# Eight batches of attention as one block without barriers, and one test of the score bound at its end

## The reference, cut to what matters

```python
q = _layernorm(q, q_gamma, q_beta); k = _layernorm(k, k_gamma, k_beta)
dots = jnp.einsum('bhnd,bhne->bhde', k, v)
out = jnp.einsum('bhnd,bhde->bhne', q, dots) * (1.0 / n)
...
scores = jnp.einsum('bhnd,bhmd->bhnm', q, k) / sqrt(Dh)
attn = jax.nn.softmax(scores, axis=-1)
sa = jnp.einsum('bhnm,bhmd->bhnd', attn, v)
```

## Time and profile before

| what | value |
|---|---|
| device time, three runs | 1817.12, 1822.64, 1822.80 us; median 1822.64 |
| the profiled execution, its span | 1855.2 us |
| TensorE, VectorE, ScalarE, POOL busy in it | 1449.7, 1112.1, 883.7, 575.7 us |
| before the first front | 18.8 us |
| front 0 | 18.8 to 130.5 us |
| attention of batches 0 to 6 | 130.5 to 1431.7 us |
| attention 7 | to 1536.2 us |
| store 7 | to 1563.5 us |
| routing and experts | to 1855.2 us |

### The profile page before, as it was taken

How to read it: one execution, slowest core, us unless ns; L and a number is a source line. 1 busy time by engine, 2 the same in 40 slices (tenths; PEclk the granted TensorE clock), 3 DMA queues, 4 the chain that set the end, 5 groups by cost and what they waited for, 6 DMA issues and landing times. The chain is left out here.

```text
span 1855.2 us, 28644 instructions
## 1 busy us (share of the span) xinstructions
PE 1449.7 (78%) x10308; PEld 902.9 (49%) x10308; DVE 1112.1 (60%) x2276; ACT 883.7 (48%) x1281; POOL 575.7 (31%) x1142
## 2 busy tenths in 40 slices
PE   5669998989698969996999699969998995213565
PEld 3435655555455536554655465536555554112444
DVE  3226765666476747564667476657665884764553
ACT  2235564656465636564656466646565772000111
POOL 1303410452035203520352035204520221035664
PEclk7788998999899989998999899989999997557777
DMA  2152015101610161005300630053004303012221
GB/s 73 36 120 63 1 40 134 56 1 37 143 51 1 29 144 58 1 6 141 85 1 1 138 92 1 1 127 102 2 1 108 99 2 98 0 44 81 90 89 60
DMA packets 73757, 109.47 MB, mean 59 GB/s; under 512 B 12410, under 2 KB 56443, under 8 KB 73595
## 3 DMA queue, kind: packets, MB, share of 16 engines
q1 hardware_dynamic: 66409, 90.47, 19.6%
q0 software_dynamic: 6144, 16.79, 2.8%
q10 hardware_dynamic: 1042, 0.01, 0.0%
HBM read 20.98 MB, written 25.43 MB: 25 GB/s over the span
## 5 line engine op out<-in xcount | busy, mean ns | idle before, releaser
L843 ACT ACTIVATE probs<-scores 128x1024 f32<-128x1024 f32 x512 | 519.3, 1023 | 265.0 <-PE scores L622 171.7
L622 PE MATMUL scores<-query_stack,key_stack 128*128 128x256 f32 x2048 | 410.5, 325 | 110.4 <-issue 86.0
L1062 DVE TENSOR_TENSOR prob_sum<-prob_sum,probs 128x512 f32<-128x512 f32 x640 | 454.8, 759 | 16.2 <-ACT probs L843 16.2
L622 PEld LDWEIGHTS scores<-query_stack,key_stack 128*128 128x128 f32 x2048 | 294.8, 196 | 256.8 <-issue 188.0
L640 PE MATMUL acc<-probs,v_sb 128*32 128x256 f32 x4096 | 331.0, 396 | 8.8 <-ACT probs L843 8.8
L862 POOL TENSOR_TENSOR attn_T<-acc_sb 128x256 f32<-128x256 f32 x64 | 61.9, 966 | 645.8 <-DVE acc_sb L1047 634.2
L663 PE MATMUL shared<-w_sb,chan 128*128 128x512 f32 (+1 forms) x512 | 188.6, 504 | 5.0 <-DVE chan L974 5.0
L1047 DVE RECIPROCAL acc_sb<-acc_sb 128x256 f32<-128x256 f32 x64 | 111.6, 1744 | 107.6 <-ACT acc_sb L833 107.6
L1182 PE MATMUL y_ps<-w_sb,zT 128*128 128x256 f32 x256 | 90.1, 488 | 76.8 <-DVE result L1341 51.4
L1351 ACT ACTIVATE zT<-zT_ps 128x256 f32<-128x256 f32 x64 | 24.6, 384 | 257.4 <-PE zT_ps L1173 209.3
L640 PEld LDWEIGHTS acc<-probs,v_sb 128*32 128x32 f32 x4096 | 88.4, 109 | 111.6 <-issue 43.0
(11 more groups left out here) (164 smaller groups left out, 2046.4 us busy)
## 6 DMA issues: line engine op xcount, KB each, us to landing
query_stack<-hi SPq DMA_DIRECT2D x128, 128.0 KB, 2.5
key_stack<-hi SPq DMA_DIRECT2D x128, 128.0 KB, 2.6
x_sb<-in_x_dram SPq DMA_DIRECT2D x8, 1024.0 KB, 8.2
key_stack<-lo SPq DMA_DIRECT2D x64, 128.0 KB, 2.5
query_stack<-lo SPq DMA_DIRECT2D x64, 128.0 KB, 2.5
v_sb<-v_next SPq DMA_DIRECT2D x16, 512.0 KB, 3.7
out_dram<-resid SPq DMA_DIRECT2D x16, 512.0 KB, 3.3
tokens_scratch<-resid SPq DMA_DIRECT2D x16, 512.0 KB, 4.2
```

Source lines behind the costliest of these rows:

```text
L622: last = pe.matmul(score_ps[u % 2][:, QB * r:QB * (r + 1)], key_stack[:, HG * g + r, P * kt:P * (kt + 1)], query_stack[:, HG * g + r, QB * ...
L843: act.activation(probs[:, u % 3, :], score_ps[u % 2][:, :], ACT.Exp, scale=DH ** -0.5) \
L1062: dve.tensor_tensor(total[:, part], probs[:, (u - 1) % 3, part] if kt == 1 else total[:, part], probs[:, u % 3, part], ALU.add).then_inc(s ...
```

## The change

All segments stand in one block. A Segment says which batch it attends to, which front and which store run beside it; lay_out deals the steps of every segment over its 64 slots and numbers the units on over all batches (0 to 511). build_segments makes the code of all engines from this plan: written out for the eight batches, without a loop. Semaphores count on over the batches, where they had been cleared. What the barrier had kept apart is now kept apart by waits: the first scores of a batch for its copies of group 0, SP's copies of group 1 for the last weighing of the batch before, agg for attn_T, the copies of ScalarE into hi and lo for the DMAs that read them. x of the next front is loaded after lin of this one. The last block of a batch is summed, copied, inverted and divided in slots 1 to 4 of the next batch, as any other. The maxima of the norms are kept for all batches and the bound is made once, in the segment of the last store. After the block the flag is tested once, and where it is set all batches are computed again, with the shift. The three DMAs that fill rows 96 to 127 stand in the small block ahead. head_mask has one copy in place of two.

```diff
@@ -102,7 +103,7 @@
              ("square", 3, 0), ("proj", 0, 1), ("proj", 1, 1), ("norms", 3, 0), ("square", 0, 1), ("v", 0),
              ("norms", 0, 1), ("square", 1, 1), ("v", 1), ("norms", 1, 1), ("proj", 2, 1), ("v", 2),
              ("square", 2, 1), ("proj", 3, 1), ("norms", 2, 1), ("square", 3, 1), ("v", 3), ("norms", 3, 1),
-             ("rest", 2), ("bound_rows",), ("rest", 2), ("bound",), ("rest", 2)]
+             ("rest", 2)]
     wanted = {"store": store, "attend": attend, "front": front, "rest": attend and front}
     part = {k: "store" for k in store_part} | {k: "attend" for k in attend_part} | {"rest": "rest"}
     return [x for x in steps if wanted[part.get(x[0], "front")]]
...
                .then_inc(sems["stack_rows"], 1)
             dve.wait_ge(sems["stack_rows"], 3)
+
+        @block.sync
+        def _(sp):
+            sp.wait_ge(sems["stack_rows"], 3)
+            for target, source in ((key_stack[MAX_ROW:MAX_ROW + 1], one_row),
+                                   (key_stack[MAX_ROW + 1:P], zero_rows[1:P - MAX_ROW]),
+                                   (query_stack[MAX_ROW:P], zero_rows)):
+                sp.dma_start(target.bitcast(F32), source.unsqueeze(1).to_broadcast([source.shape[0], H, N])) \
+                  .then_inc(sems["stack_rows"], 16)
+            sp.wait_ge(sems["stack_rows"], 3 + 48)
 
     def ended():
 
@@ -382,39 +385,22 @@
         nc.gpsimd.sem_clear(range(nums[0], nums[-1] + 1))
         nc.all_engine_barrier()
 
-    def attended(b, **work):
-
-        needs_shift = nc.values_load(shifted[0:1, 0:1], min_val=0, max_val=1)
-        with nc.If(needs_shift > 0):
+    ended()
+    build_segments(nc, env, [Segment(front=0)] +
+                   [Segment(attend=b, front=b + 1 if b + 1 < B else None, store=b - 1 if b else None)
+                    for b in range(B)] + [Segment(store=B - 1, last=True)], first_x_loaded=True, guard=True)
+    ended()
+
+
+    needs_shift = nc.values_load(shifted[0:1, 0:1], min_val=0, max_val=1)
+    with nc.If(needs_shift > 0):
+        with nc.Fori(0, B) as b:
+            build_segments(nc, env, [Segment(front=b)], first_x_loaded=False, guard=False)
+            ended()
             build_shift(nc, env)
             ended()
-        build_batch(nc, env, b, attend=True, **work)
+            build_segments(nc, env, [Segment(attend=b), Segment(store=b)], first_x_loaded=False, guard=False)
             ended()
-
-    ended()
-    build_batch(nc, env, 0, front=True)
-    ended()
-    attended(0, front=True)
-    with nc.Fori(1, B - 1) as b:
-        attended(b, front=True, store=True)
-    attended(B - 1, store=True)
-    build_batch(nc, env, B, store=True)
-    ended()
...
+def lay_out(segments, guard):
...
+        steps = order(seg.has("attend"), seg.has("front"), seg.has("store"))
+        if not guard:
+            steps = [x for x in steps if x[0] not in ("square", "norms")]
+        elif seg.last:
+            steps = [("bound_rows",), *steps, ("bound",)]
+        dealt = (UNITS if seg.has("front") else 4 * T) if seg.has("attend") else 1
+        dealt = spread(steps, dealt) + [[]] * (UNITS - dealt if seg.has("attend") else 0)
+        for u, slot in enumerate(dealt):
...
+
+            if not first_x_loaded and all_fronts:
+                sp.dma_start(x_sb[:, :, :], env["x_v"][segments[0].front, :, :, :]).then_inc(s["x_loaded"], 16)
+            for n, seg in enumerate(segments):
+                if seg.has("attend"):
+
+                    await_count(sp, "weighed", UNITS * seg.attends)
+                    if seg.earlier_front:
+                        for h in range(2):
+                            for j in range(2, 4):
+                                await_read(sp, seg.earlier_front, "proj", j, h)
+                    copy_group(sp, env, 1)
+                    if seg.earlier_front:
+                        for k in range(T // 2 - 2, T // 2):
+                            await_read(sp, seg.earlier_front, "v", k)
+                    copy_v(1)
...
+                if seg.has("front"):
+                    if n + 1 < len(segments) and segments[n + 1].has("front"):
+                        for t in range(T - 2, T):
+                            await_read(sp, seg, "lin", t)
+                        sp.dma_start(x_sb[:, :, :], env["x_v"][segments[n + 1].front, :, :, :]) \
+                          .then_inc(s["x_loaded"], 16)
+                    if seg.has("attend"):
+                        sp.wait_ge(s["weighed"], UNITS * seg.attends + UNITS // 2)
+                    for h in range(2):
+                        for j in range(2):
+                            await_read(sp, seg, "proj", j, h)
+                    copy_group(sp, env, 0)
+                    for k in range(T // 2 - 2, T // 2):
+                        await_read(sp, seg, "v", k)
+                    copy_v(0)
+            await_count(sp, "x_loaded", 16 * (all_fronts - x_preloaded))
...
             def scores(u):
-                g, qb, kt = u // (NQB * T), u // T % NQB, u % T
-                if u == UNITS // 2:
-                    pe.wait_ge(s["group_copied1"], STACK_DMAS)
+                a, g, qb, kt = u // UNITS, u % UNITS // (NQB * T), u // T % NQB, u % T
+                if u % UNITS == 0:
+                    await_count(pe, "group_copied0", STACK_DMAS * (a + segments[0].has("front")) if all_fronts else 0)
+                if u % UNITS == UNITS // 2:
+                    pe.wait_ge(s["group_copied1"], STACK_DMAS * (a + 1))
...
                 if kind == "agg":
-                    if at[0] == T - QB // P:
-                        pe.wait_ge(s["attn_ready"], late)
+                    pe.wait_ge(s["attn_ready"], G * NQB * seg.stores + NQB * (G - 1) + at[0] // (QB // P) + 1)
                     last = product(ps[:, 0:C], [(attn_T[:, c, tok[at[0]]], waggT[:, c, :]) for c in range(CH)])
...
-                        act.wait_ge(s["group_copied1"], STACK_DMAS)
+                    ps = await_full(act, seg, *st)
+                    if at[0] == 0:
+                        await_count(act, "group_copied1", STACK_DMAS * seg.groups)
                     read(act.activation(z2T[:, :, P * at[0]:P * (at[0] + 1)],
...
-
-            if late:
-                divide(-1)
-            for u, slot in enumerate(slots):
-                for st in slot:
-                    step(st)
-                if attend and u > T and u % T == 4:
+                elif kind == "head_scale" and at[0] < seg.pool_quarters:
+                    scale_heads(pool, seg, at[0]).then_inc(s["head_scaled"], 1)
+
+            for n, slot in enumerate(plan):
+                u = slot.unit
+                if units and u is None and n and plan[n - 1].unit == units - 1:
+                    divide(units // T - 1)
+                for st in slot.steps:
+                    step(*st)
+                if u and u > T and u % T == 4:
                     divide(u // T - 1)
 
```

More of the change, by code:

```diff
@@ L25 @@
 from contextlib import ExitStack
+from dataclasses import dataclass, field
 F32 = mybir.dt.float32
@@ L67, in spread @@
     rests = sum(x[1] for x in steps if x[0] == "rest")
-    share = sum(WORK[x[0]] for x in steps if x[0] != "rest") / (slots - rests)
+    share = sum(WORK[x[0]] for x in steps if x[0] != "rest") / (slots - rests) or 1.0
     done, out = 0.0, [[] for _ in range(slots)]
@@ L122, in bank_uses @@
 def bank_uses(slots):
-    return {s: k for k, s in enumerate(s for slot in slots for s in slot if s[0] not in BANKLESS)}
+    return {s: k for k, s in enumerate(s for slot in slots for s in slot if s[1][0] not in BANKLESS)}
 def hybrid_kernel(nc, x, w0, q_gamma, q_beta, k_gamma, k_beta, w1, wagg, bagg, wgate, wexp, out):
@@ L505, in _, with has, groups @@
                 pool.wait_ge(s[f"max_row_in{g}"], 16)
-def build_batch(nc, env, b, front=False, attend=False, store=False):
-    s = env["sems"]
-    nxt = b + 1 if attend else b
-    steps = order(attend, front, store)
-    dealt = (UNITS if front else 4 * T) if attend else 1
-    slots = spread(steps, dealt) + [[]] * (UNITS - dealt if attend else 0)
-    use = bank_uses(slots)
+@dataclass(eq=False)
+class Segment:
+    front: object = None
+    attend: object = None
+    store: object = None
+    last: bool = False
+    fronts: int = 0
+    attends: int = 0
+    stores: int = 0
+    scaled_before: int = 0
+    scaled_last_before: int = 0
+    pool_quarters: int = 0
+    slots: list = field(default_factory=list)
+    earlier_front: object = None
+    def has(self, part):
+        return {"front": self.front, "attend": self.attend, "store": self.store}[part] is not None
+    @property
+    def groups(self):
+        return self.attends + self.has("attend")
@@ new lines @@
+@dataclass(eq=False)
+class Slot:
+    unit: object
+    steps: list
+def lay_out(segments, guard):
+    fronts = attends = stores = scaled = scaled_last = 0
+    earlier_front = None
+    plan = []
+    for seg in segments:
+        seg.fronts, seg.attends, seg.stores = fronts, attends, stores
```

(40 more changed lines are left out.)

464 lines of the change are left out of this document (219 added, 245 removed).

## The result

| | before | after |
|---|---|---|
| device time, median of 12 runs each (lowest to highest) | 1826.26 us (1817.12 to 1831.94) | 1837.14 us (1832.53 to 1838.51) |
| ratio, 95% interval | | 1.0059 (1.0042 to 1.0075) |
| span of the profiled execution | 1855.2 us | 1833.3 us |

The changed kernel is 10.9 us slower; forecast was 16.9 us faster. The direction is wrong, and the forecast is 28 us off.

A forecast was written before the change was run, and what follows sets the result against it. TensorE was taken to set the pace in the attention. The terms +65.5 + 24.6 + 5 - 81.0 - 21 - 7 - 3 = -16.9 took 1822.6 us to 1805.7, range 1795 to 1817.

The forecast's parts named there:

- the start: Ahead of the first front: waiting for the three DMAs that fill stack rows moves it from 18.87 to 84.3, +65.5 us.
- the gaps: Seven boundaries between batches: barrier, clearing, flag load and branches leave the path before the scores, -81.0 us.
- agg 6: TensorE's step in slot 5, batches 1 to 6: waits 4.1 us each for POOL's division of attn_T, +24.6 us.
- the drain and the fresh start: Around each of seven batch boundaries: work running out and starting anew goes, 3 us each (0 to 5), -21 us.
- the new deal: Steps dealt over 64 slots with four fewer of rest, said to give the filling at boundaries; no size of its own.
- The first attention and front 0: Batch 0's scores need only the front's last copies, and the wait for x falls away: -7 us (0 to -10).
- The end: Flag loaded and branched on once after the last store, +5 us; one score bound and no barrier there, about -3.
- The copies on SP: Copies into the stacks for the next batch: group 0 costs 0, group 1 costs 0, up to 3 us a batch.

The follow-up runs named there:

- rests_back: The changed kernel with 6.8 slots without steps at the end of a batch instead of 2; 1824.35 us, 0.9995 of the kernel before.
- rests_close: The changed kernel with 6.8 slots without steps and each batch's last query block closed in slots 0 and 1 of the next; 1802.99 us.
- before_unrolled: The kernel before with its loop over batches 1 to 6 written out, barriers, flag and branches kept; 1774.96 us, 0.9734 of the kernel before.
- rows_32: The changed kernel with key_stack's rows 96 to 127 filled by one transfer of 32 partitions instead of 1 and 31; 1781.44 us.

## Why the prediction was wrong

**Right: the start.** +65.5 forecast, +66.0 in the profile, 65 and 67 in the two kernels that price it. The reading of the earlier trace rows (one engine, landing near 84) holds.

**Right: the gaps.** -81.0 forecast; all seven are gone, and writing out the loop gives 48.5 us in ordinary runs, where the profile has 51.5.

**Right as a mechanism, wrong in this kernel: agg 6.** The prediction said "The place of agg 6 (slot 5) and the work ahead of it stay." Only the first half holds. 24.6 forecast, 24.8 with the old deal, 4.2 in after.

**The step that failed: batches 1 to 6.** The step is the term of 3 us a boundary for "the drain and the fresh start", together with the new deal of the steps, which stood at nothing in the sum. Forecast for these batches: six gaps (81.0 less the 6.55 before batch 1, 74.5), six times 3 us of drain and fresh start, and the 24.6 of agg 6: -67.9. Measured: -39.9. These 28.0 us are the error (26.5 in profile time over all, -16.9 against +9.6). They come in two parts:

- *Drain and fresh start, -21 for seven boundaries (-18 for six).* With the old deal (rests_back) batches 1 to 6 shrink by 46.3 us; gaps and the wait for attn_T give -74.5 + 24.8 = -49.7. So what is left for the term is +3.4, not -18: 21.4 us missed. Its lower bound of 0, "if the work merely moves", was nearer. No run shows the 3 us a boundary, which were my estimate; what the runs showed in their place is this remainder.

  The +3.4 is a remainder and holds other waits that came and went: TensorE's for POOL's lo (20.4 us before) are gone, its waits for probs grew from 24.2 to 47.4. In sum its idle time beside the gaps and the wait for attn_T stayed the same (73.1 before, 1077.0 - 979.0 - 24.8 = 73.2), and its busy time rose by 3.3 us instead of falling.

  With the wait at agg 6 removed as well (rests_close) the remainder is +4.9 (-69.6 against -74.5). There TensorE's busy time did fall, by 12.1 us (975.7 to 963.7), so the clock does come back (0.99 in the batch shown; 0.94 and 0.97 in those of before, gaps included). But its idle time without the gaps rose by 16.9 us (before 1123.3 - 975.7 - 74.5 = 73.1; rests_close 1053.7 - 963.7 = 90.0), at exps that wait for VectorE's sums (TensorE's waits for probs 53.7 us, where they were 24.2) and at VectorE's resid and lin_out (15.4 and 17.0).

  In after the busy time didn't even fall (980.9): the granted clock was 0.51 in two stretches of batch 3, nearly as low as the 0.50 behind a gap of the kernel before (497.76 to 499.76 us). The first begins behind the wait of 2.21 us before agg 5, the second at the end of the wait of 5.25 us for POOL's lo:

```profile
735.30:742.20 6.90, 6.27 (x31) 3.98 (x30) 5.06 (x15) 3.02 (x4) 1.46 (x2) 0.51 0.99 282
...
817.20:820.70 3.50, 3.33 (x18) 2.22 (x19) 0.62 (x1) 2.18 (x3) 0.07 (x1) 0.51 0.00 0
```

- *The new deal, 0 in the sum.* I had written that fewer slots of rest give "the filling". They gave collisions: 6.4 us in batches 1 to 6 and 4.6 in batch 0, 11.7 in the runs. That is a net figure, since the new deal took 20.6 us off the wait for attn_T and put other waits in its place. Named and tested is one, POOL's lo: 20.4 us before, 31.6 after, 18.0 with resid moved. The waits for VectorE's resid (2.9 to 15.2) and norm_max (0.9 to 10.3) grew as well; they weren't tested one by one, so which of them the rest of the loss goes through is open.

**The first attention and front 0:** -7 forecast, with the gap and the drain before batch 1 -16.6. Front 0 gave 6.6 and batch 0 gave 11.9: -18.5. The end (+5 - 3) measures +2.0.

**The copies on SP:** as forecast, no wait. The last issue of group 0 ends at 888.96; with 2.5 us to land, that is 5 us ahead of the scores at 896.96 that need it. Those of group 1 begin 3.1 us into the batch, and ScalarE's z2T at 744.34 waits for TensorE, not for them:

```profile
719.97 0.53 SPq L413 DMA_DIRECT2D query_stack<-hi  x1
...
888.37 0.59 SPq L415 DMA_DIRECT2D key_stack<-hi  x1
...
744.34 0.38 ACT L844 ACTIVATE hi<-shared 128x256 f32<-128x256 f32 x1 [2.79 <-PE shared L718]
```

Still open: how the 17 us of new idle time in rests_close divide over its waits, and why the straight boundaries of before_unrolled cost half from the fourth on.

## What to carry to other kernels

When a barrier between stages goes, count the gap that the trace shows; a gain for "drain and warm-up" has to be worked out from the waits that will be left. Here it came to nothing: the work that stood at the edges moved inside and met other work there, and a granted clock of 0.51 came again behind its waits. When steps are dealt out by their share of the slots, removing a rest moves every step; look at each queue where two engines meet (here one division and two resid steps ahead of a scaling) before saying that a place stays. And a transfer that was hidden has to be priced at full before it is put ahead of a barrier; here a later wait made it harmless, and one row more left 14.7 us of its 66.

## What the runs showed of the hardware

- Broadcast copies inside SBUF: 31 partitions of 32 KB ran at about 18 GB/s with a share of 0.06, one DMA engine (after, 22 to 57 us); 32 partitions at 184 GB/s with a share of 0.99, all 16 (rows_32, 24 to 30 us). That is about 11.5 GB/s for each engine (184 / 16) when all run, less than the one engine reached alone.
- Writing out the loop gave 48.5 us in the runs. In the profile its five long gaps (13.3 to 14.2 us) became 2.8 to 5.9, 48.1 us less together or 9.6 each, and the straight boundary before batch 7 fell by 3.3, from 6.11 to 2.83.
- One profiled execution (before) had 31.5 us more in a stage of 64 gathers, matmuls and scatters than that of after in the same code, spread over waits of several engines, much of it with no releaser (17.6 us of TensorE's before y_ps, 21.1 of ScalarE's before zT and 16.1 of VectorE's before result, with none of these in after). A difference between two profiles is to be held against the runs stage by stage.
